# First loads reordered, four tiles' roots computed by VectorE, and causal masks written by sixteen 32 x 32 products

## The reference

```python
x = x + _L0_xattn_ref(_layernorm(x), ctx_1024, ...)   # l0x: attention to a context, 8 heads of 64
x = x + _L0_ffn_ref(_layernorm(x), ...)               # l0f: causal self-attention, 16 heads of 64; l0m: 32 experts
x = x + _L1_xattn_ref(_layernorm(x), ctx_1024, mask)  # l1x: 16 heads of 8
x = x + _L1_ffn_ref(_layernorm(x), ...)               # l1f: causal self-attention, 16 heads of 8; l1m: 8 experts
...                                                   # l2x, l2m, l3x, l3m

def causal_attention(q, k, v, scale):                 # in l0f and in l1f
    scores = jnp.einsum('bhqd,bhkd->bhqk', q, k) * scale
    causal = jnp.tril(jnp.ones((s, s), dtype=bool))
    scores = jnp.where(causal, scores, -jnp.inf)      # l1f: the lowest float instead of -inf
    attn = jax.nn.softmax(scores, axis=-1)
    return jnp.einsum('bhqk,bhkd->bhqd', attn, v)
```

## Time and profile before

| | us |
|---|---|
| median of three runs | 1353.68 |
| the profiled execution's own time | 1355.32 |
| its span, first to last instruction | 1353.5 |
| PE busy | 1165.6 |
| DVE busy | 989.8 |
| ACT busy | 876.4 |
| POOL busy | 561.8 |

### The profile page before, as it was taken

One profiled execution on the slowest core, in us unless ns is written; L12 is line 12 of the kernel. 1 busy time (PEld: TensorE's weight loads), 2 busy tenths in 40 slices (PEclk: granted clock), 3 DMA queues, 4 the chain that ended last, 5 costly groups with the idle time before them and its releaser, 6 DMA issues.

```text
span 1353.5 us, 29885 instructions
## 1 busy us (share of the span) xinstructions
PE 1165.6 (86%) x9611; PEld 894.9 (66%) x9654; DVE 989.8 (73%) x2220; ACT 876.4 (65%) x2403; POOL 561.8 (42%) x671
## 2 busy tenths in 40 slices
PE   3899889999997999997888888888999988997824
PEld 2677677777775688885666666655788666666503
DVE  3566767676676899997777766667666787887787
ACT  2666456655554799996877776663566546775584
POOL 5800266666652322246222231131877516882100
PEclk9999999999999999998999999998999999998967
DMA  8000000000000666660000010002322017750001
GB/s 286 20 10 9 21 2 2 0 0 0 0 2 10 206 214 211 212 210 16 2 0 0 1 43 0 0 2 82 115 86 82 0 39 193 190 152 1 1 0 31
DMA packets 37956, 83.08 MB, mean 61 GB/s; under 512 B 5330, under 2 KB 19026, under 8 KB 37748
## 3 DMA queue, kind: packets, MB, share of 16 engines
q1 hardware_dynamic: 37876, 82.07, 19.5%
HBM read 80.40 MB, written 1.64 MB: 61 GB/s over the span
## 4 chain that ended last, share of the span: by engine, by line
PE 61%; ACT 15%; DVE 13%; issue 7%; SPq 2%; POOL 2%; DMA 1%; DVEq 0%; ACTq 0%; POOLq 0%
PE score_bank L1630 17%; ACT h_all L1075 11%; PE f_bank L1664 6%; PE score_bank L1491 6%; PE f_bank L1401 4%; PE turn_bank L1507 4%; PE turn_bank L1664 3%; PE out_bank L1547 3%; PE out_bank L1664 3%; PE out_bank L1516 2%; SPq L569 2%; PE score_bank L1475 2%; DVE top_score L1971 2%; PE f_bank L1424 1%; PE out_bank L1556 1%
## 5 line engine op out<-in xcount | busy, mean ns | idle before, releaser
L1075 ACT ACTIVATE h_all<-score_bank,top_score 128x128 f32<-128x128 f32 x896 | 277.4, 402 | 117.2 <-DVE top_score L1971 117.2
L1630 PE MATMUL score_bank<-parts 128*128 128x512 f32 x1040 | 297.3, 403 | 11.5 <-DVE h_parts L2177 8.1
L1630 PEld LDWEIGHTS score_bank<-parts 128*128 128x128 f32 x1040 | 192.8, 191 | 76.7 <-DVE h_parts L2177 18.8
L1971 DVE TENSOR_REDUCE top_score<-score_bank 128x4 f32<-128x512 f32 x224 | 143.0, 681 | 129.8 <-PE score_bank L1491 129.8
L2177 DVE TENSOR_TENSOR h_parts<-score_bank,h_parts 128x512 fp32r<-128x512 f32 x260 | 178.0, 685 | 1.9 <-ACT h_parts L1190 1.9
L1190 ACT ACTIVATE h_parts<-score_bank 128x512 fp32r<-128x512 f32 x260 | 155.7, 599 | 33.2 <-DVE score_bank L2161 8.7
L758 POOL TENSOR_TENSOR small<-small,half_neg 128x4 f32<-128x4 f32 (+4 forms) x25 | 37.6, 1509 | 196.7 <-DVE small L1944 84.2
L1507 PE MATMUL turn_bank<-CF,h_all 128*128 128x128 f32 x512 | 81.7, 282 | 33.6 <-DVE work L1983 21.8
L783 POOL TENSOR_TENSOR h_all<-h_all,prob_rec 128x512 f32<-128x512 f32 x64 | 66.6, 1049 | 70.6 <-DVE prob_rec L1975 70.3
L1507 PEld LDWEIGHTS turn_bank<-CF,h_all 128*128 128x128 f32 x512 | 55.2, 141 | 60.3 <-DVE work L1983 17.3
L2149 DVE TENSOR_TENSOR score_bank<-work,score_bank 128x512 f32<-128x512 f32 x124 | 86.3, 696 | 9.6 <-ACT score_bank L1167 4.7
(11 more groups left out here) (408 smaller groups left out, 2617.0 us busy)
## 6 DMA issues: line engine op xcount, KB each, us to landing
work<-gates_l0m SPq DMA_DIRECT2D x62, 512.0 KB, 3.7
W0X<-gates_l2m SPq DMA_DIRECT2D x32, 256.0 KB, 3.7
CTX<-gates_l2m SPq DMA_DIRECT2D x32, 256.0 KB, 3.7
wset<-in_l0m SPq DMA_DIRECT2D x32, 128.5 KB, 3.4
W0X<-gates_l1m SPq DMA_DIRECT2D x8, 512.0 KB, 3.8
wset<-in_l1m SPq DMA_DIRECT2D x8, 384.0 KB, 4.4
CTX<-gates_l1m SPq DMA_DIRECT2D x6, 512.0 KB, 4.0
big<-in_w0f SPq DMA_DIRECT2D x4, 512.0 KB, 8.1
```

Of the source, the lines that this page charges most:

```text
L1075: last = act.activation(held[c][:, P * m:P * m + P], score_bank[c][:, P * m:P * m + P], ACT.Exp, bias=top_score[c][:, m:m + 1], **sums)
L1630: last = pe_.matmul(bk[:, :], wt, y[:, x], start=(part == 0), stop=(part == len(parts_of) - 1))
L1971: dve.tensor_reduce(top_score[c][:, :], split(score_bank[c][:, :], HEADS), AX_X, ALU.max, negate=True)\
```

## The change

First, the loads. X's first four batches get a semaphore of their own (in_x4); the constants and the context tile of batch 0 follow; W0X is loaded in two pieces (three quarters, and the part for the output product with in_w0o); BOX and the later twelve batches of X come behind. All other loads are handed out one group per batch inside the loop that loads context tiles, each behind that batch's context tile. Second, the roots of batches 0 to 3 are computed by DVE with four Newton steps; the measures of the other twelve batches move behind the first stage's Y jobs, and POOL roots only those. POOL's first memsets move ahead of its root. Third, PE runs twelve products of a memset tile at its start. Fourth, ACT's sines move from behind batch 0 to behind batch 2. Fifth, each causal fill is one product of 2 columns and sixteen products with 32 rows, 32 outputs and 512 columns, into the four banks; the mask is laid out so that group c of 32 partitions holds all four quarters of its rows.

```diff
-            load(X[:, 0:4, :], a["x"][0:4].rearrange("b s d -> s b d"), in_x)
-            load(X[:, 4:B, :], a["x"][4:B].rearrange("b s d -> s b d"), in_x)
+            load(X[:, 0:4, :], a["x"][0:4].rearrange("b s d -> s b d"), in_x4)
             load(CF[:, :], a["cf"], in_c)
             load(VEC[:, :], a["vec"], in_c)
             load(BROW[:, :], a["brow"], in_c)
-            load(BOX[:, :], rows_to_all(a["brow"][:, 0:P]), in_c)
...
+            context0(0, 0)
+            load(W0X[:, 0:3, :], split(a["w0x"][:, 0:3 * BANK], 3), in_w0x)
+            context0(0, 1)
+            load(X[:, 4:B, :], a["x"][4:B].rearrange("b s d -> s b d"), in_x)
+            load(BOX[:, :], rows_to_all(a["brow"][:, 0:P]), in_x)
+            load(W0X[:, 3, :], a["w0x"][:, 3 * BANK:4 * BANK], in_w0o)
...
+            pieces = {2: lambda: weights0("qa"), 3: lambda: weights0("ka"), 4: lambda: weights0("v"), 5: lambda: weights0("o")}
...
+            for b in range(2, B):
+                for job in (2, 3):
+                    r, k = place(front_at["l0x"], 4, b // 2 - 1, b % 2, job)
+                    sp.wait_ge(f_full[r], k + 1)
+                context0(b // 2, b % 2)
+                if b in pieces:
+                    pieces[b]()
...
-            power("l0x")
...
+            power("l0x", 1)
...
-            two_layers(act, "ACT", "l0x", attention(LAYERS[0]), "l0f", attention(LAYERS[1]), after={("l0x", 0): sines})
+            two_layers(act, "ACT", "l0x", attention(LAYERS[0]), "l0f", attention(LAYERS[1]), after={("l0x", 2): sines})
...
                         if causal:
-                            for bk in banks:
-                                pe_.matmul(bk[:, :], ident_bf, causal_bf, start=True, stop=False, skip_group_check=True)
+
+                            pe_.matmul(banks[0][:, 0:2], ident_bf, own_bf[:, 0:2], start=True, stop=True, skip_group_check=True)
+
+                            for j in range(4):
+                                for c, bk in enumerate(banks):
+                                    rows = slice(32 * c, 32 * c + 32)
+                                    pe_.matmul(bk[32 * j:32 * j + 32, :], ident_bf[rows, 32 * c:32 * c + 32],
+                                               causal_bf[rows, P * j:P * j + P].unsqueeze(1).to_broadcast([32, HEADS, P]),
+                                               start=True, stop=False, skip_group_check=True)
...
-            pe_.wait_ge(in_c, 16 * 4)
-            pe_.wait_ge(in_w0x, 16)
+            pe_.wait_ge(step("setup.warm"), 1)
+            for _ in range(12):
+                pe_.matmul(out_bank[:, :], ones_bf[:, :], ones_bf[:, :].unsqueeze(1).to_broadcast([P, 4, P]), start=True, stop=True)
+            pe_.wait_ge(in_c, 16 * 3)
...
-            dve.wait_ge(in_x, 16 * 2)
-            for b in range(B):
+            dve.wait_ge(in_x4, 16)
+            for b in range(4):
                 measure(X, b)
             variances("l0x", 0)
-            variances("l0x", 1)
+
+            x, y, t = ve[:, 0:4], r1[:, 0:4], t0[:, 0:4]
+            dve.wait_ge(varied, 1)
+            link(dve.tensor_scalar(y.bitcast(I32), x.bitcast(I32), 1, None, ALU.logical_shift_right))
+            link(dve.tensor_scalar(y.bitcast(I32), y.bitcast(I32), -1, 0x5f3759df, ALU.mult, ALU.add))
+            for n in range(4):
+                link(dve.tensor_tensor(t, y, y, ALU.mult))
+                link(dve.scalar_tensor_tensor(t, t, -0.5, x, ALU.mult, ALU.mult))
+                last = dve.scalar_tensor_tensor(y, t, 1.5, y, ALU.add, ALU.mult)
+                if n < 3:
+                    link(last)
+            last.then_inc(rooted, 1)
             powered("l0x", 0)
+
+            def later_tokens():
+                dve.wait_ge(in_x, 16 * 2)
+                for b in range(4, B):
+                    measure(X, b)
+                variances("l0x", 1)
...
-                       ahead={("l0x", B - 2): lambda: variances("l0f", 0), ("l0f", B - 1): lambda: variances("l0m", 0),
+                       ahead={("l0x", 0): later_tokens, ("l0x", 2): lambda: powered("l0x", 1),
+                              ("l0x", B - 2): lambda: variances("l0f", 0), ("l0f", B - 1): lambda: variances("l0m", 0),
...
-                       after={("l0x", 0): lambda: powered("l0x", 1), ("l0x", B + 1): lambda: variances("l0f", 1),
+                       after={("l0x", B + 1): lambda: variances("l0f", 1),
```

More of the change, by code:

```diff
@@ L600, in _ @@
                     load(last_row[n], a["w0f"][P - 1:P, 1024 * at:1024 * at + 1024].partition_broadcast(P), in_w0f)
-            load(CTX[:, :, :], a["ctx"].rearrange("b s d -> s b d"), in_w1)
-            load(W1X[:, :], a["w1x"], in_w1)
-            load(W1F[:, :], a["w1f"], in_w1)
-            load(WL2[:, :], a["wl2"], in_w1)
-            with sp.Fori(1, PAIRS) as i:
-                for s in range(2):
-                    for job in (2, 3):
-                        r, k = place(front_at["l0x"], 4, i - 1, s, job)
-                        sp.wait_ge(f_full[r], k + 1)
-                    context0(i, s)
+            context0(0, 0)
@@ new lines, in shared @@
+            def shared():
+                load(CB[:, 0:P], a["cb"][:, 0:P], in_rows)
+                load(CB[:, P + BANK:], a["cb"][:, P + BANK:], in_rows)
+                for c in range(4):
+                    load(causal_bf[32 * c:32 * c + 32, :].rearrange("p (j k) -> p j k", j=4),
+                         a["cb"][:, P:2 * P].rearrange("(j x) k -> x j k", j=4), in_rows)
+                load(BOX1[:, :], rows_to_all(a["brow"][:, 2 * P:3 * P]), in_rows)
+                load(CROW[:, :], rows_to_all(a["brow"][:, P:2 * P]), in_rows)
@@ new lines, in routers, with places @@
+            def routers():
+                load(RB[:, :], rows_to_all(a["l0m_rb"]), in_rows)
+                load(LB[:, :], rows_to_all(a["l2m_bias"]), in_rows)
+                for g in range(CHUNKS):
+                    load(B2[32 * g:32 * g + 32, :], a["b2"], in_rows)
+                load(RW[:, 0:39], a["rw"], in_rows)
+                load(RWB[:, :], a["rwb"], in_rows)
+            def places():
+                load(POSI[:, :], rows_to_all(a["pos"]), in_rows)
+                load(MASKU[:, :], rows_to_all(a["mask"]), in_rows)
@@ L616, in _ @@
                     for table, at in ((cosq1, 4 + j % 2), (sinq1, 4 + j // 2)):
-                        load(table[rows, :], a["cf"][32 * g:32 * g + 8, P * at:P * at + P], in_turns)
+                        load(table[rows, :], a["cf"][32 * g:32 * g + 8, P * at:P * at + P], in_w1)
             sp.wait_ge(step("l0f.weights"), 3)
@@ L754, in power @@
                         continue
+                    if name == "l0x":
+                        pool.wait_ge(rooted, 1)
                     pool.wait_ge(varied, part_at[name] + part + 1)
@@ L1418, in front_job @@
                         if u == 2:
+                            if isinstance(i, int) and 2 * i + s == 0:
+                                pe_.wait_ge(in_w0x, 16)
                             pe_.wait_ge(cT_ready[t], 16 * (s // 2 + 1) + 16 * i)
@@ L1553, in unit_step @@
                         pe_.wait_ge(gathered, B + 2 * s + 2 + 4 * i if n == "l0f" else s + 1 + 2 * i)
+                        if n == "l0x" and isinstance(i, int) and 2 * i + s == 0:
+                            pe_.wait_ge(in_w0o, 16 * 3)
                         count, w = (4, W0X[:, 3, :]) if n == "l0x" else (8, w0f["o"])
```

50 lines of the change are left out of this document (22 added, 28 removed).

## The result

The changed kernel takes 1335.32 us, the median of four runs (1329.38 to 1340.28), against 1353.23 us (1351.64 to 1354.75, four runs) before: ratio 0.9855, 95% interval 0.9835 to 0.9875, 18 us or 1.5% faster. The forecast was 1334.0 (1327 to 1349).

A forecast was written before the change was run, and what follows sets the result against it. It took a mostly PE chain of waits to bound the kernel, with causal fills 2% of it and stalls at the start. Start 8.1 plus fills 11.6 made 19.7 us, from 1353.7 to 1334.0 us, range 1327 to 1349.

The forecast's parts named there:

- First tile: Part 1, start of the kernel: y_tok at 8.2 instead of 14.50, 6.2 us earlier; bounds 4.7 and 6.5.
- W0X, the worry of this part: Load PE's first product waits for: could be late next; expected at 8.5 to 9.5, needed at 9.5.
- Warm products: Part 2, PE in batch 0: twelve products ahead bring slow groups to full clock, 1.0 us, between 0 and 1.8.
- the bound of 1.8: Most that warm products could win: two groups of batch 0 were slow, so at most 1.8 us.
- Context tile: Part 3, batch 2 of l0x: its tile is issued a stage ahead, so PE's stall goes, 7.3 us before the sines.
- Sines and reload: Part 4, ACT behind batch 2: sines cost 2.65, four more table loads in the loop 3.6 to 4.2; 6.4 us lost.
- The angles: Input of ACT's sines: ready at 35, ACT there at about 37; the 2 us slack covers it.
- The start: Parts 1 to 4 together: 6.2 + 1.0 + 7.3 - 6.4 = 8.1 us gained, bounds 4 and 13.
- Fills: Part 5, causal fills of l0f and l1f: 0.38 saved per fill, 32 fills, 95% passing, 11.6 us.
- my lower bound of 0.47: Shortest time taken for one causal fill: 0.47 us, saving 0.49 per fill, 15.6 us.
- My estimate of 0.52 us per fill: Causal fill by the skill's 4 ns per further tile: 0.52 us, making the part 13 us.

The follow-up runs named there:

- warm0: The changed kernel with none of the twelve products at PE's start; 1336.27 us, ratio to before 0.9841.
- after_again: The changed kernel once more, unchanged, on a third chip; 1335.52 us, ratio to before 0.9832.
- reload_once: The changed kernel with one more exponential, of one column into an unused tile, behind the sines; 1333.81 us, ratio to before 0.9834.
- combo: The changed kernel with a dummy exponential behind the sines, AO in four POOL instructions and 21 products at PE's start; 1330.92 us, ratio to before 0.9827.
- fill_only: The kernel before with only the causal fills changed to small products, plus the loads that lay out their mask; 1345.93 us, ratio to before 0.9931.
- start_only: The changed kernel with the four full-width fills and the mask loaded whole; 1351.47 us, ratio to before 0.9961.

## Why the prediction was right

**First tile.** Forecast y_tok at 8.2 and 6.2 us; it came at 8.65, 5.85 us earlier. X's first part landed at 3.95, not 3.6, and the step from there to y_tok took 4.70 against 4.6. W0X, the worry of this part, landed at 9.4 (issued at 3.04, 6.4 to landing), just in time.

**Warm products.** Forecast 1.0 between 0 and 1.8. S0's lead over before beyond y_tok's is 0.42 in the profiled execution (6.27 - 5.85); against no products it is 1.14 (warm0). In after_again the lead at S0 is 7.95, and all groups were fast. Against no products the mean of the six profiles with twelve is 1.4, and the bound of 1.8 was too low, since without them a third group is slow too (2.07 in warm0). The mean was fairly placed, for a term that varies from one execution to the next.

**Context tile.** Forecast 7.3. S1 to S2 went from 15.24 to 9.70, so 5.5. This is the step that failed: I costed AO only as time ahead of the sines, not as a neighbour of DVE. In before, AO ran from 18.14 to 22.66 while DVE had nothing to do there; the earlier start moved DVE's products of batch 0 into it. Of the 1.7 us between 9.70 and the forecast's 8.0, that hold is 1.1 and a stretch at the lower clock 0.6 (reload_once 9.08, combo 7.96).

**Sines and reload.** Forecast 2.65 and 3.6 to 4.2. S3 to S4 took 10.55 against 8.05, 2.5; the loop's loads 3.45 (reload_once). That the first term fits so well is luck of the one execution: in the nine other kernels and executions with the sines behind batch 2, S3 to S4 took 11.30 to 11.73, so 3.3 to 3.7 more, and each of them has a stretch at the lower clock between 42.3 and 49.8 us that after hasn't. The lower clock behind the sines had no term in my sum. The angles were ready at 34.74 (35 forecast) and cost nothing. A warning that stood only in the order of the instructions, a load inside a loop's body, was worth a term of its own.

The start sums to 5.85 + 0.42 + 5.54 - 2.50 - 2.96 = 6.35; the lead at S15 is 6.30. (The last term is S4 to S15, 91.71 against 88.75; it is less than 3.45 because before's passes were 0.5 slower than those of reload_once.)

**Fills.** Forecast 0.38 each and 11.6 in all; measured 0.49 each and 14.6 in all (14.5 in fill_only). Two terms were mis-sized. The issue of sixteen products, 0.12 in my sum, takes 0.05: they start within that. And from the 2-column product to the first small one are 0.10, not 0.15. The rest was right: from the start of the last small product to the first score product are 0.315 (0.215 + 0.09 in my sum). The three make the 0.46 measured, close to my lower bound of 0.47. Nearly all of it passed: 14.6 of 32 x 0.49 = 15.7, 93% against 95% forecast. A batch of l0f goes from 15.16 to 14.66 (S28 to S29), while S17 to S18 is 16.1 in both, so in some batches the fill is off the path.

The Trainium skill, TensorEngine Tiling (Key Properties), says that a change of tiling mode drains the engine. The trace agrees as far as it goes: the step out of the small products is 0.10 (0.315 - 0.215), as the one out of the full fill was before, and the step into them is at most the 0.10 from the 2-column product on; what of either is a drain no row tells. The Trainium skill, TensorE: Matmul & The Clock Gate (Measured speedup vs the span model), gives some 4 ns for each further tile; here fifteen further ones take 50 ns, 3.3 each. My estimate of 0.52 us per fill by that figure stood nearer to the 0.46 than my own sum.

**What was not in the sum.** Of 20.9 us gained (6.3 + 6.6 + 8.0), 18.4 are left. The loss is where both kernels have the same instructions, and the granted clock shows it: at the start of l1x S32 to S33 took 9.15 instead of 8.20, with the lower level from 613.6 for 17.1 us (before: from 627.4 for 10.2), and behind S63 after took 453.63 against 451.80, with 76 us at the lower level against 72. Two executions of the kernel after show how large this is (the columns are those of the rows on the clock above). After, then after_again, 390 to 410 us:

```profile
390.00:410.00 20.00, 13.87 (x134) 11.10 (x130) 10.56 (x43) 9.78 (x39) 7.47 (x7) 1.00 0.00 1
```

```profile
390.00:410.00 20.00, 14.27 (x92) 11.75 (x91) 7.52 (x26) 8.56 (x37) 6.41 (x5) 0.60 0.00 1
```

S31 to S32 takes 233.71 in the first and 239.72 in the second, and after_again gets nearly as much back behind S63 (448.50 against 453.63), so that both spans are 1335. Of the ten profiles with the new fills five have such a stretch of 17.1 us there and S31 to S32 at 239.7 to 239.8, and five have none and 233.7 to 233.9. The runs of one kernel order themselves by the clock: after took 1340.28 us at 0.957 and 1329.38 at 0.969. So the right total is in part luck: the start's missing 1.8 and the 2.5 lost to the clock were mostly made up by the 3.0 that the fills gave beyond the forecast. Whether the change itself shifts the stretches of lower clock, or only one execution against the next, is settled in part: S32 to S33 is 9.15 to 9.24 in all ten profiles with the new fills (fill_only too), 8.78 in start_only and 8.20 in before, and the lower level holds there for 17.1 us in those ten, for 13.7 in start_only and 10.2 in before. That speaks for a shift that comes with the new fills, by some 1 us; the rest behind S63, from 447.0 to 453.6 in these ten, varies from one execution to the next.

## What to carry to other kernels

When a stage starts earlier, lay its instructions over what the other engines do in the same microseconds, not only over its own waits: a long GpSimd instruction that was free because VectorE had nothing to do beside it can hold VectorE for up to its length once VectorE has, and cutting it into pieces bounds the hold. Read from the order of instructions where a table load or another implicit instruction ends up: in a loop's body it runs every pass, and one dummy instruction ahead of the loop takes it out. A block mask or another fill with short contraction is worth cutting into 32 x 32 products, which stream side by side.

## What the hardware did that I had not expected

GpSimd (POOL) can hold VectorE (DVE), and which instruction is held depends on both. Held until POOL's end (0.1 to 0.6 us behind it) were h_all (a product of two SBUF tiles) beside TENSOR_TENSOR (4.55, 3.73) and CAST (2.07), and y_tok beside TENSOR_TENSOR (2.40) and once beside TENSOR_SCALAR (1.20 in after, from 49.44). h_all beside TENSOR_SCALAR was not held (0.69 at 45.92 in after, with POOL at L941 from 44.77 to 47.61). The Trainium skill, SBUF — State Buffer (Who interferes with whom), has the rule: the two share one pair of ports, and a VectorE instruction with two SBUF inputs and a GpSimd instruction that reads SBUF don't run side by side; whichever issues second waits for the whole of the first. The traces agree for h_all beside TENSOR_TENSOR and CAST, with the 4.55 us beside it. They agree the other way round too: in after the CAST of the mask, which began at 71.10 behind an h_all that had begun at 70.93, took 2.35 instead of 1.89. The 0.69 beside a TENSOR_SCALAR, which reads SBUF too, doesn't follow from the rule, and y_tok, which reads one tile, isn't covered by the rule for two inputs; the same section says that a tensor_scalar can take the shared ports too, in a mode of two ports, and no run here tells whether it did. Weighed against the moved instructions, that rule would have found the hold by AO, 1.1 of the missing 1.7 us.

The kernel before had shown it in one row that I didn't read, the maximum of that line: h_all at 63.25 took 1.37 instead of 0.69, beside the mask's conversion. Timeline of before, POOL and DVE:

```profile
62.17 1.91 POOL L927 CAST MASK<-MASKU 128x2048 bf16<-128x2048 uint8 x1
63.25 1.37 DVE L1979 TENSOR_TENSOR h_all<-h_all,prob_rec 128x512 f32<-128x512 f32 x1
```

Sixteen products of 32 x 32 with 512 columns each take 0.43 us from the first start to the last end, against 0.385 for one, in either order of the groups. Twelve warm products with PE idle for 1.5 to 2.5 us behind them kept the clock through batch 0's products in one execution, the one with the longest idle time (2.53), and not in five others; 19 or 21 with less than 0.5 us of idle time behind them kept it there in three of three. A table load takes 1.283 us each time, also when the set is there already.
